# Attention of a DiT block: units in one sequence over both batches, each unit preparing one tile ahead, batch 1's normalisation spread over units

## The reference, cut to what matters

```
mod = swish(c) @ w_mod + b_mod              # shift, scale, gate for attention and MLP
xn  = ln(x) * (1 + sc_msa) + sh_msa
q, k, v = split(xn @ w_qkv + b_qkv)         # 16 heads of 36
q, k = ln(q) * g_q, ln(k) * g_k             # per head
o   = softmax(q @ k.T * 36**-0.5) @ v       # 2048 x 2048 per head and batch
x   = x + g_msa * (o @ w_proj + b_proj)
xn2 = ln(x) * (1 + sc_mlp) + sh_mlp
out = x + g_mlp * (gelu(xn2 @ w1 + b1) @ w2 + b2)
```

## Time and profile before

| | |
|---|---|
| median of 3 runs | 3115.08 us (3113.78 to 3118.76) |
| the profiled execution, as timed | 3116.54 us |
| its span, first to last instruction | 3114.7 us, mean TensorE clock 0.950 |
| busy PE, DVE, ACT, POOL | 91%, 65%, 50%, 20% |
| modulation and batch 0's preparation | 0 to 194.8 us |
| attention of batch 0 (first exponential to last matmul) | 194.8 to 1044.0 us |
| preparation of batch 1 | 1044.0 to 1168.5 us |
| attention of batch 1 | 1168.5 to 2019.4 us |
| projection and MLP | 2019.4 to 3114.7 us |

### The profile page before, as it was taken

One profiled execution on the slowest core, in us unless ns is written; L12 is line 12 of the kernel. 1 busy time (PEld: TensorE's weight loads), 2 busy tenths in 40 slices (PEclk: granted clock), 3 DMA queues, 4 the chain that ended last, 5 costly groups with the idle time before them and its releaser, 6 DMA issues. The chain is left out here.

```text
span 3114.7 us, 47318 instructions
## 1 busy us (share of the span) xinstructions
PE 2823.2 (91%) x14764; PEld 1451.3 (47%) x14764; DVE 2025.6 (65%) x2637; ACT 1561.6 (50%) x2203; POOL 628.1 (20%) x452
## 2 busy tenths in 40 slices
PE   4669999999999569999999999926999999999999
PEld 1334444444434234444444434313756657657566
DVE  5558878878889748878878879846353443443521
ACT  2457767767777547767767768723111121121110
POOL 0243333333310043323423321001000000000000
PEclk9789999999999789999999999967999999999999
DMA  5131111111100221111111110054012021021100
GB/s 162 59 65 31 28 26 32 32 26 32 32 15 14 69 54 27 27 32 26 32 26 32 32 23 14 16 190 134 21 62 72 11 82 59 24 82 33 50 16 16
DMA packets 198484, 141.40 MB, mean 45 GB/s; under 512 B 149990, under 2 KB 150502, under 8 KB 198258
## 3 DMA queue, kind: packets, MB, share of 16 engines
q1 hardware_dynamic: 196712, 136.97, 16.2%
q10 hardware_dynamic: 1676, 3.02, 0.3%
HBM read 77.53 MB, written 28.85 MB: 34 GB/s over the span
## 5 line engine op out<-in xcount | busy, mean ns | idle before, releaser
L631 DVE TENSOR_TENSOR at_plo<-at_p 128x1024 fp32r<-128x1024 f32 x1024 | 1257.9, 1257 | 269.0 <-ACT at_p L548 254.8
L548 ACT ACTIVATE at_p<-at_ps 128x1024 f32<-128x1024 f32 x1024 | 1049.0, 1029 | 438.9 <-PE at_ps L762 438.3
L776 PE MATMUL at_ps<-at_plo,at_vr 128*37 128x512 f32 x2048 | 1071.8, 592 | 0.0
L773 PE MATMUL at_ps<-at_p,at_v 128*73 128x512 bf16 x2048 | 797.8, 390 | 10.3 <-DVE at_plo L631 10.3
L762 PE MATMUL at_ps<-at_qkT 109*128 x2048 | 626.8, 389 | 78.1 <-DMA at_qkT<-at_stk 50.8
L1204 PE MATMUL ml_ps<-ml_w2s,ml_hid 128*128 128x288 f16 x3456 | 429.8, 287 | 2.0 <-issue 2.0
L1225 PE MATMUL ml_ps<-ml_xhi,ml_w 128*128 128x512 f16 x1296 | 400.6, 382 | 12.2 <-ACT ml_g L1055 9.3
L1204 PEld LDWEIGHTS ml_ps<-ml_w2s,ml_hid 128*128 128x128 f16 x3456 | 338.8, 98 | 87.8 <-issue 2.5
L773 PEld LDWEIGHTS at_ps<-at_p,at_v 128*73 128x73 f16 x2048 | 233.3, 114 | 250.1 <-DVE at_plo L631 13.3
L776 PEld LDWEIGHTS at_ps<-at_plo,at_vr 128*37 128x37 f32 x2048 | 234.1, 114 | 222.6 <-issue 1.2
L762 PEld LDWEIGHTS at_ps<-at_qkT 109*128 (+1 forms) x2048 | 137.3, 99 | 401.0 <-issue 362.1
(11 more groups left out here) (145 smaller groups left out, 2269.0 us busy)
## 6 DMA issues: line engine op xcount, KB each, us to landing
head_sums<-at_oT SPq DMA_DIRECT2D x256, 72.0 KB
ml_held<-head_sums SPq DMA_DIRECT2D x64, 256.0 KB
at_xin<-in_x SPq DMA_DIRECT2D x8, 1152.0 KB, 5.4
ml_x<-in_x SPq DMA_DIRECT2D x8, 1152.0 KB, 5.6
out<-ml_x SPq DMA_DIRECT2D x7, 1152.0 KB, 4.5
wm<-in_L_cond_w_mod SPq DMA_DIRECT2D x6, 1152.0 KB, 14.1
ml_hid<-in_L_cond_w SPq DMA_DIRECT2D x5, 1152.0 KB, 5.7
ml_held<-head_rden SPq DMA_DIRECT2D x24, 216.0 KB
```

Source lines behind the costliest of these rows:

```text
L548: act.activation(p[:, s % NP, :], ps[:, 2 * (s % 2):2 * (s % 2) + 2, :].rearrange("p a n -> p (a n)"), ACT.Exp).then_inc(exp_done, 1)
L631: nc.vector.tensor_tensor(plo[:, s % NP, :], p[:, s % NP, :], high, ALU.subtract).then_inc(plo_ready, 1)
L773: nc.tensor.matmul(acc[0:VW, bass.ds((unit % 2) * CH, CH)], v16[:, h % 2, 2 * s + a, 0:VW], high, start=(s == 0 and a == 0), stop=False, s ...
L776: last = nc.tensor.matmul(acc[0:RW, bass.ds((unit % 2) * CH, CH)], vr[:, h % 2, 2 * s + a, 0:RW], plo[:, s % NP, a * CH:(a + 1) * CH], sta ...
```

## The change

The 8 groups of both batches now stand in one sequence of 128 units, `U` = 0 to 127, with the group number `G` a constant of the program text (8 copies of the group's code on PE, ACT and DVE; SP and POOL have all 128 units written out).

- **One tile ahead.** Unit U handles tile U+1, not tile U; tile X belongs to group X // 16 + 1. Tile 0 is made in the preparation of batch 0. So there are 112 tiles (before 96), 111 of them in units; the 16 added ones (X = 48 to 63) are those of batch 1's first group, which before were made in that batch's preparation. 17 units have no tile (before 32).
- **No drain.** The last three sums of a group are made in the first three steps of the next, `tile_high` and `tile_low` have no copy at a group's end, and `keys_ready` is gone: the first scores of a group wait for tile 16G - 1, which was handled two units earlier.
- **`traw` is gone.** ACT squares and DVE scales straight from `tile_bank`; the products of the next tile therefore wait for `t_yn`, the end of L641 (now L683), no longer for `t_raw`.
- **Batch 1's normalisation in the units of batch 0.** Group 0: in each unit SP loads 128 tokens of batch 1 into `xy`, DVE takes `bn_stats` twice at step 4 and `bn_aggr` at step 5. Group 1: SP loads them again, POOL subtracts the mean and multiplies (L555), copies the 64 tail columns (L557), SP stores the rows to DRAM (`y_dram`). Group 2: SP loads the rows, PE transposes 4 blocks at step 4 and one at step 7 into `hat_bank`, ACT applies shift and scale at steps 5 and 7 (L595) and writes `xhi` at step 7, DVE writes `xlo` at step 7 (two instructions).
- **The first unit** waits for the DMA transposes of the chunk of keys that each pair of steps needs, not for all 16.
- `oT` has one slot instead of two; `v32` of the first tile of a group goes to row 0 of the other half at a group's end.

Where the names differ: L776, L773, L762 become L845, L842, L833; L789 becomes L861; L548, L538, L566 become L616, L589, L583; L631, L638, L641, L650 become L705, L679, L683, L692.

The statistics stand between the sum of squares and the scaling that PE now waits for. The core of the diff, by engine (loops over `b` and the old `group` functions are what the removed code consisted of, and are left out):

```diff
 # SP
+            for stored in tq_stored:
+                sp.wait_ge(stored, 16 * TPC * NCH // 2)
+            def unit(G, u):
+                U = G * UNITS + u
+                if G == STATS_IN:
+                    sp.wait_ge(n_mv, u + 1)
+                    sp.dma_start(xy[:, 0:H], xf[bass.ds(N + u * P, P), :]).then_inc(n_loaded, 16)
+                if G == Y_IN:
...
+                    sp.wait_ge(n_stored, 16 * u + 16)
+                    sp.dma_start(xy[:, 0:H], xf[bass.ds(N + u * P, P), :]).then_inc(n_loaded, 16)
+                if G == HATS_IN:
...
+                    sp.wait_ge(n_lo, u + 1)
+                    sp.dma_start(xy[:, :], y_dram[bass.ds(u * P, P), :]).then_inc(ny_loaded, 16)
+                if G < GROUPS - 1:
+                    sp.wait_ge(t_low, U + 2)
+                    sp.wait_ge(t_high, 2 * U + 3)
+                    sp.dma_start_transpose(qkT[(G + 1) % 2][:, :, bass.ds(u * P, P)],
...
+                if U:
+                    store_sums((U - 1) // UNITS, (U - 1) % UNITS)
+                if G == Y_IN:
+                    sp.wait_ge(n_whole, u + 1)
+                    sp.dma_start(y_dram[bass.ds(u * P, P), :], xy[:, :]).then_inc(n_stored, 16)
 # POOL
+            tile_power(0)
+            for U in range(GROUPS * UNITS):
+                G, u = U // UNITS, U % UNITS
+                if G == Y_IN:
...
+                    pool.wait_ge(n_loaded, 16 * (NT + u + 1))
+                    pool.tensor_scalar(xy[:, 0:H], xy[:, 0:H], nmv[:, u, 0:1], nrstd[:, 1, u:u + 1], ALU.subtract, ALU.mult).then_inc(n_y, 1)
+                    pool.wait_ge(n_y, u + 1)
+                    pool.tensor_copy(xy[:, H:KC * P], xy[:, KF * P:H]).then_inc(n_whole, 1)
+                if U + 1 < TILES:
+                    tile_power(U + 1)
+                if u % NCH == 2 and U // NCH + 1 < B * NH:
+                    head(U // NCH + 1)
 # ACT
-                        act.copy(traw[:, :, :].rearrange("p e d -> p (e d)"), tile_bank[:, 0:2 * GW]).then_inc(t_raw, 1)
-                        act.activation(txc[:, :, :], traw[:, :, :], ACT.Square).then_inc(t_sq, 1)
+                act.activation(txc[:, :, :].rearrange("p e d -> p (e d)"), tile_bank[:, 0:2 * GW], ACT.Square).then_inc(t_sq, 1)
+                    if G == HATS_IN and s == 5:
+                        hats(u, range(KF))
+                    if G == HATS_IN and s == 7:
+                        hats(u, (KF,))
+                        hats_high(u)
 # DVE
-                        nc.vector.scalar_tensor_tensor(out=txc[:, :, :], in0=traw[:, :, :], scalar=HD ** 0.5, in1=bcast(tssq[:, 1, :], 2, HD),
+                nc.vector.scalar_tensor_tensor(out=txc[:, :, :], in0=tile_bank[:, 0:2 * GW].rearrange("p (e d) -> p e d", e=QK), scalar=HD ** 0.5,
+            tile_normal(0)
 # PE
-                    pe.wait_ge(t_raw, X + 1)
+                    pe.wait_ge(t_yn, X + 1)
+            tile_products(0, 0, 1, range(0, 14))
+                    if first and s % 2 == 0:
+                        pe.wait_ge(tq_stored[(s // 2) % 2], 16 * TPC * (s // 4 + 1))
+                    if fixed and u == 0 and G and s == 0:
+                        pe.wait_ge(t_stored, 16 * G * NT + 16)
+                    elif not first:
+                        sums(U - 1, (h - 1) % GH if fixed and qc == 0 else h, s - LAG + STEPS)
+                    if fresh and s < 2:
+                        tile_products(U + 1, 0 if at_end else u + 1, G + (2 if at_end else 1), range(7 * s, 7 * s + 7))
+                    if G == HATS_IN and s == 4:
+                        hat_turns(u, range(KF))
+                    if G == HATS_IN and s == 7:
+                        hat_turns(u, (KF,))
```

747 lines of the change are left out of this document (389 added, 358 removed).

## The result

| | before | changed |
|---|---|---|
| median of 4 runs each | 3116.1 us | 2976.6 us (2975.9 to 2976.9) |
| ratio, with its 95% interval | | 0.9553 (0.9541 to 0.9565) |
| span of the profiled run | 3114.7 us | 2974.1 us |
| mean TensorE clock | 0.950 | 0.972 |
| first exponential to last matmul of attention | 194.8 to 2019.4 us | 181.8 to 1880.7 us |

139.5 us faster; the forecast was 131, with 2971 to 3014 as its range. Which terms carry the eight microseconds between is the question from here on.

The account below looks back on a forecast made before the run. TensorE was taken to set the pace inside a group. Terms -124.5 - 56 - 6 + 38.4 + 12 + 5 = -131 us, off the median 3115.1, gave 2984 us; own range 2972 to 2996, wider range 2971 to 3014.

Parts of the forecast that it names:

- The gap between the batches: Between batch 0's last matmul and batch 1's first exponential: 124.5 us disappears, while 15 more tiles return 38.4 us.
- The group ends: At six group ends: the drain, half clock included, disappears, 9.3 us each, 56 us in all.
- rival D: At the group ends: a wait still drains PE, seven ends of up to 9.3 us, 3049 us; chance 0.03.
- The first unit: Start of attention: first scores need only chunk 0, second exponential at 191.4 us; gain 6 us, ends 3 and 8.
- The sign that I had named: PE through attention: a granted clock of 1.00 from the first unit to the last would show the prediction right.
- The statistics: Group 0, DVE between sum and scaling: bn_stats and bn_aggr add 0.3 us a unit, 5 us; ends 0 and 15.
- The transposes: Group 2, PE: five transposes of normalised rows add 0.75 us a unit, 12 us; ends 10 and 21.
- Groups 1 and 2 beside PE: POOL, ACT and DVE work in groups 1 and 2 costs nothing; uncovered, bounded by 24 us.
- rival B: Groups 1 and 2 not free: POOL's scaling delays the chain or ACT is late; 8 to 24 us; chance 0.13.
- The new wait: Every unit with a tile: products wait for the scaling's end; room 0.4 us, costed at nothing in a plain unit.
- rival A: Every unit: the wait for the scaling doesn't hold, costing 11 to 55 us, likeliest time 3005 us; chance 0.14.
- Reading PSUM: DVE's scaling and ACT's square: estimated some 0.06 us later and 0.04 us earlier, so the room would hold.

Follow-up runs that it names:

- e6: Changed kernel without batch 1's normalisation and its transfers in groups 0 to 2; attention distance 1684.19 against 1698.91 us, ratio to the kernel before 0.9522.
- e1: Changed kernel with the old group's last three sums made before the new group's first scores; attention distance +10.7 us, ratio to the kernel before 0.9595.
- e2: Changed kernel with sums first and PE waiting for the oT store at seven group starts; attention distance +38.4 us, ratio to the kernel before 0.9701.
- e7: Changed kernel with the first scores waiting for all 16 transposes; start +12.1 us, attention distance -2.8 us, ratio to the kernel before 0.9589.
- e4: Changed kernel with group 0's statistics moved behind the scaling, to step 7; attention distance +0.1 us, ratio to the kernel before 0.9555.
- e11: Changed kernel with tile 0's power before POOL's first head and group 0's statistics at step 7 except its last unit; ratio to the kernel before 0.9541.
- e8: Changed kernel with two extra DVE sums ahead of each scaling, delaying it; attention distance +63.7 us, ratio to the kernel before 0.9758.

## Why the prediction was right, and where it was off

- **The gap between the batches** (-124.5, with the tiles -88.7 in its interval): -90.4. The mechanism and the size hold. PE's 2.56 us for a tile holds too: units with a tile take 13.46, those of group 7 10.84 to 10.92 but for the last. The 124.5 us end at batch 1's first exponential, where the clock was still 0.50 for another 3.55 us. That alone is 1.8 us, about what the interval gave more; no run separates it.
- **The group ends** (6 x 9.3): in the three intervals where they stand with nothing but tiles (4, 5, 6) -30.7 against -30.5. Measured against e6, whose groups 0 to 2 hold nothing but tiles either, the six were worth 9.8, 8.2, 8.9, 9.5, 9.8 and 9.0 us, 55.0 in all against 56. I had one distance, from group 0, for six ends. Group 1's was worth 1.6 less, and its half clock was 3.2 us shorter, which is 1.6 us. That the drains go was right everywhere (rival D falls), and e1 and e2 show that parts of the drain cost 1.5 and 5.5 us. That the rest of the 9.3 was the longer wait for the tile's transpose is read from the rows of before; no run puts that wait back.
- **The first unit** (-6, ends -3 to -8): -10.0 in the first line of the table, 2.5 of it preparation, so -7.5; e7 gives 7.2 for the wait alone. The second exponential was forecast for 191.4 and came at 188.35, or 2.5 later with the old preparation: 190.9. The sign that I had named, a granted clock of 1.00 from the first unit on, holds only from 188.6 us; up to there it was 0.50. The step's chain was right, POOL ahead of the scaling ahead of the products; its add took 0.72 and its power 2.03 us instead of 1.11 and 2.50, with fewer instructions of DVE beside them:

```profile
182.18 2.03 POOL L527 TENSOR_TENSOR at_tssq<-at_tssq,power 128x8 f32<-128x8 f32 x1
184.24 0.46 DVE L683 SCALAR_TENSOR_TENSOR at_txc<-at_ps,at_tssq 128x288 f32<-128x288 f32 x1 [1.53 <-POOL at_tssq L527]
184.76 0.90 PE L861 MATMUL at_ps<-wq,at_xhi 128*128 128x432 f16 x2 [15.93 <-DVE at_txc L683]
188.35 1.02 ACT L616 ACTIVATE at_p<-at_ps 128x1024 f32<-128x1024 f32 x1 [2.84 <-PE at_ps L833]
```

- **The statistics** (+5, ends 0 to 15): +1.2 by e6. This is the term that was mis-sized most. I added DVE's 0.94 us to a chain whose length POOL sets, and took POOL's part as it was. It got shorter:

```profile
234.81 1.11 POOL L525 TENSOR_TENSOR at_tssq<-at_tssq,head_eps 128x8 f32<-128x8 f32 x1 [4.87 <-DVE at_tssq L679]
235.78 0.81 DVE L715 BATCH_NORM_STATS2 at_ssq<-at_xy 128x6 f32<-128x288 f32 x2
236.00 1.64 POOL L527 TENSOR_TENSOR at_tssq<-at_tssq,power 128x8 f32<-128x8 f32 x1
236.51 1.21 DVE L705 TENSOR_TENSOR at_plo<-at_p 128x1024 fp32r<-128x1024 f32 x1
```

The power takes 1.64 us where one `plo` runs beside it, as here, and 2.50 to 2.52 where two do. With `bn_stats` in DVE's queue POOL is done 0.86 us sooner, and the scaling no longer waits for POOL but for DVE's own row. e4 and e11 confirm it from the other side: with the statistics out of the way the power is 2.50 us again, DVE waits 0.33 us for it, and the unit is only 0.1 us shorter. The Trainium skill (SBUF — State Buffer, "Who interferes with whom") says that a VectorE instruction with two SBUF inputs and a GpSimd instruction that reads SBUF exclude each other, and that one with one SBUF input does not contend. `plo` has two and `bn_stats` one; the trace agrees in direction, by the 1.64 and 2.50 us. It shows the delay on one side only, since `plo` itself takes 1.20 to 1.26 us beside the power.
- **The transposes** (+12): by their own rows 80 x 0.11 = 8.8 us. I had priced one at 0.15 us, from a row that holds the latency of the last.
- **Groups 1 and 2 beside PE** (0, rival B 8 to 24): group 1 0.0, though POOL's scaling took 2.3 to 4.2 us and its queue was 65% busy; group 2 4.7 us. Rival B's mechanism, ACT late and the scaling behind it, is real in every unit of group 2, and over half of its lower price. That group 2 as a whole came out at 13.5 us against 12 is luck in part: the transposes were put 3.2 us too high, and the wait beside them at nothing.
- **The new wait** (room 0.4 us, rival A): 0.17 to 0.22 us of room in a plain unit, 0.3 in each fourth, by e8 and by the rows. I took the whole 0.28 us of the removed copy plus 0.13 as room. But 0.13 us between the scaling's end and the products was no room: where PE waits, 0.16 us pass there. Rival A would have begun at 0.2 us, half of what I thought. A wait of the products for the scaling was my own sign that the prediction is wrong, and it came, in group 2 and, by a tenth of a microsecond, in the units of group 0. It cost about 6 us there and nothing in the 79 other units with a tile, so the forecast held.
- **Reading PSUM.** DVE's scaling takes 0.44 to 0.46 us from PSUM in all 112 rows, and took 0.46 in all 96 from SBUF. ACT's square takes 0.40 from PSUM (0.41 to 0.43 in eight rows) and took 0.46 from SBUF. The Trainium skill (VectorE: DVE Perf Modes, "The TRN2 errata") has PSUM slower for VectorE and faster for ScalarE; the trace agrees for ScalarE and shows no penalty for VectorE in this instruction. Where the two differ the measurement decides, and the sum had left it out.
- **The balance.** The spans differ by 140.6 us, 9.6 more than forecast. 4.3 of that are the preparation and what follows attention, which vary from run to run; by the lines of the table, and to rounding, group 0 gave 4.2 more than forecast (3.8 the statistics, all but 0.3 of them here), the start 1.8 beyond its preparation, the gap between the batches 1.7, groups 4 to 7 together 0.7; the interval of group 1 gave 1.0 less and that of group 2 1.9 less. The two dominant terms, which came from distances measured over the whole of a gap, were right within 2%. The terms that I built from single instructions were off by a fifth (the first unit), a quarter (the transposes) and three quarters (the statistics), and one that I put at nothing was 4.7 us; all are small beside the two. The forecast's own range of 2972 to 2996 doesn't come out of the ends of its three terms, which give 2975 to 3006.
